# Weight preparation on three engines, centring products inside the GRU's last cells, and two alternating products in the last layer of a graph network kernel

## The reference

```python
agg = _prop_once(x, edge_attr, src, dst, ...) + _prop_once(x, edge_attr, dst, src, ...)
    # _prop_once: segment_sum(mlp3(concat(x[from], x[to], edge)), to), hidden width 256
s1 = _gru(x, agg, ...); s2 = _gru(agg, s1, ...); s3 = _gru(s1, s2, ...)
x = _layernorm(x + s3)
X = x
for l in range(3):
    S = segment_sum(X[src], dst)
    Z = (1.0 + eps[l]) * X + S
    H = relu(Z @ W1[l] + b1[l])
    X = H @ W2[l] + b2[l]
x = _layernorm(x + X)
```

## Time and profile before

| | us |
|---|---|
| median of 3 runs | 2313.74 (2311.68 to 2316.02) |
| the profiled execution | 2316.54 |
| its span | 2314.8 |
| busy PE / DVE / ACT / POOL | 2257.0 / 1762.0 / 1231.7 / 1182.7 |
| edge stage, from the span's start | about 1899 |
| GRU and first layer norm, until line 2136 starts | to 2025.9 |
| three layers and second layer norm | to 2314.8 |

### The profile page before, as it was taken

How to read it: one execution, slowest core, us unless ns; L and a number is a source line. 1 busy time by engine, 2 the same in 40 slices (tenths; PEclk the granted TensorE clock), 3 DMA queues, 4 the chain that set the end, 5 groups by cost and what they waited for, 6 DMA issues and landing times.

```text
span 2314.8 us, 38789 instructions
## 1 busy us (share of the span) xinstructions
PE 2257.0 (98%) x12559; PEld 1831.4 (79%) x12559; DVE 1762.0 (76%) x4035; ACT 1231.7 (53%) x2118; POOL 1182.7 (51%) x858
## 2 busy tenths in 40 slices
PE   4999999999999999999999999999999999899997
PEld 3888888888888888888888888888888874587775
DVE  7888888888888888888888888888888856703112
ACT  4565666566666656665666566656656543411122
POOL 2566666666566656665666666666656640001100
PEclk9999999999999999999999999999999999999999
DMA  4356454455445554554554445444545339286965
GB/s 163 71 113 125 98 106 92 88 112 101 91 89 106 99 98 91 108 97 89 100 112 93 88 98 107 99 89 104 101 89 99 72 62 268 94 351 258 384 263 189
DMA packets 242547, 292.52 MB, mean 126 GB/s; under 512 B 126757, under 2 KB 200056, under 8 KB 234385
## 3 DMA queue, kind: packets, MB, share of 16 engines
q1 hardware_dynamic: 168194, 236.50, 33.9%
q0 software_dynamic: 73216, 54.58, 18.0%
q10 hardware_dynamic: 1040, 0.52, 0.1%
HBM read 218.43 MB, written 73.08 MB: 126 GB/s over the span
## 4 chain that ended last, share of the span: by engine, by line
PE 92%; DMA 3%; DVE 2%; issue 1%; ACT 1%; POOL 0%; DVEq 0%; SPq 0%; POOLq 0%; ACTq 0%
PE bank L1238 24%; PE bank L1224 18%; PE bank L1250 16%; PE bank L2136 8%; PE bank L1303 4%; PE bank L1282 4%; PE bank L1298 4%; PE bank L1185 4%; DMA l_ring<-adj 2%; PE bank L1801 2%; PE bank L1267 2%; PE bank L1809 1%; PE bank L1268 1%; PE bank L2150 1%; PE bank L2159 1%
## 5 line engine op out<-in xcount | busy, mean ns | idle before, releaser
L495 POOL DMA_INDIRECT sums<-outb,target x416 | 667.3, 1604 | 590.8 <-ACT outb L666 456.8
L488 POOL DMA_INDIRECT xg<-in_x,gidx x416 | 489.3, 1176 | 148.3 <-issue 137.1
L1250 PEld LDWEIGHTS bank<-w3t,h 128*128 128x128 f32 x3328 | 387.5, 192 | 8.8 <-issue 0.2
L1250 PE MATMUL bank<-w3t,h 128*128 128x128 f32 x3328 | 388.3, 275 | 0.1
L1238 PE MATMUL bank<-h1h,w2h 128*128 128x512 f32 x832 | 365.5, 439 | 3.3 <-DVE h1l L861 3.3
L648 ACT ACTIVATE h<-bank,b2c 128x512 f32<-128x512 f32 x416 | 286.2, 688 | 122.2 <-PE bank L1238 122.2
L634 ACT ACTIVATE h1h<-hpre 128x512 fp32r<-128x512 f32 x416 | 257.8, 628 | 171.9 <-DVE hpre L857 171.9
L1238 PE MATMUL bank<-h1h,w2l 128*128 128x512 f32 x832 | 328.8, 395 | 0.0
L1238 PE MATMUL bank<-h1l,w2h 128*128 128x512 f32 x832 | 328.5, 395 | 0.0
L861 DVE SCALAR_TENSOR_TENSOR h1l<-hpre,h1h 128x512 fp32r<-128x512 f32 x416 | 268.6, 687 | 16.8 <-ACT h1h L634 16.8
L857 DVE TENSOR_TENSOR hpre<-pb,bank 128x512 f32<-128x512 f32 x416 | 264.9, 676 | 2.3 <-PE bank L1224 2.1
(11 more groups left out here) (263 smaller groups left out, 3695.6 us busy)
## 6 DMA issues: line engine op xcount, KB each, us to landing
l_ring<-adj SPq DMA_DIRECT2D x54, 1568.0 KB, 8.2
rowb<-along SPq DMA_DIRECT2D x104, 512.0 KB, 4.4
ef<-in_edge_attr SPq DMA_DIRECT2D x103, 256.0 KB, 2.7
adj<-band SPq DMA_DIRECT2D x46, 480.0 KB
adj<-band SPq DMA_DIRECT2D x23, 540.0 KB
stay<-adj SPq DMA_DIRECT2D x6, 1568.0 KB, 14.8
xg<-in_x,gidx POOLq DMA_INDIRECT x416
sums<-outb,target POOLq DMA_INDIRECT x416, 4.0
```

The lines of the kernel that those rows point to most:

```text
L488: pool.indirect_dma_start(out=to, out_offset=None, in_=a["x"], in_offset=bass.IndirectOffsetOnAxis(ap=ids, axis=0)).then_inc(s_x[par], 16)
L495: pool.indirect_dma_start(out=tables[k % 2], out_offset=bass.IndirectOffsetOnAxis(ap=target[par][:, 1, k:k + 1], axis=0), in_=outb[par][:, ...
L1250: last = nc.tensor.matmul(bank[6 + way][:, t * P:(t + 1) * P], h2[:, way, k, t * P:(t + 1) * P], w3t[:, k, :], start=not bias and k == 0, ...
```

## The change

Four edits. **Start:** `whalf` is computed by GpSimd ahead of its branch; ScalarE copies the upper parts and `w3t`, VectorE only subtracts; the four operations on `b3` go to the other program, which does not run here. In the windowed program SyncE loads `xw` ahead of `rowb`; VectorE does `sums(0)` and `lower_parts(0)` ahead of `pair_rows`, and `nodes(0)` and `compare(0)` behind `ways(0)`. **GRU:** the centring product of group n-2 stands in the last GRU's cell n, between its `h` products and its `hn`; it goes to bank 3 or 7, the one that `hn` of the cell before used, and ScalarE squares it and copies it to `x1` at once. Variance, root and scaling follow, the scaling now within `x1`; group 3 is scaled by GpSimd, group 5 by ScalarE. **Last layer:** TensorE alternates `unit(n)` (the first product of chunk n) with `second(n-1)`. **Store:** SyncE stores groups 0 and 1 apart.

```diff
-HALVES = ((0, 16, (0, 1, 2, 3)), (16, NB, (4, 5, 6)))
+NORMED = ((0, 16, (0, 1, 2, 3)), (16, NB, (4, 5, 6)))
...
                 for g in range(2):
+                    window(g, g)
                     everywhere(g, g)
-                for g in range(2):
-                    window(g, g)
...
+            pool.wait_ge(s_wload, 6 * 16)
+            for f in range(HB):
+                nc.gpsimd.tensor_tensor(whalf[:, f, 0, :], w1n[:, f, 0:D], w1n[:, f, D:2 * D], ALU.add).then_inc(s_wsum, 1)
+                nc.gpsimd.tensor_tensor(whalf[:, f, 1, :], w1n[:, f, 0:D], w1n[:, f, D:2 * D], ALU.subtract).then_inc(s_wsum, 1)
+            pool.wait_ge(s_wsum, 2 * HB)
+            nc.gpsimd.tensor_scalar(whalf, whalf, 0.5, None, ALU.mult).then_inc(s_whalf, 1)
...
+            for f in range(HB):
+                act.wait_ge(s_wT, 3 + f)
+                nc.scalar.copy(w1h[:, f, :, :].rearrange("p j m -> p (j m)"), bank[2 + f][:, 0:3 * P]).then_inc(s_wh, 1)
...
                 onehot(0, 0, 0)
                 window(0, 0)
+                sums(0)
+                lower_parts(0)
                 pair_rows()
-                sums(0)
-                nodes(0, 0, early=True)
-                lower_parts(0)
-                compare(0, 0, 0)
                 onehot(1, 1, 0)
                 window(1, 1)
                 ways(0)
+                nodes(0, 0, early=True)
+                compare(0, 0, 0)
...
+    def middle(j):
+        return bank[6 if j == NGR - 1 else 7 if j % 2 == 0 else 3]
...
+            if c == LAYERS - 1 and n >= 2:
+                square(n - 2)
             act.wait_ge(s_pre, seq + 1)
...
+            nc.scalar.activation(sqr[0:r, j % 2, 0:n], middle(j)[0:r, 0:n], ACT.Square).then_inc(s_sqd, 1)
+            nc.scalar.copy(x1[0:r, b:b + nb, :], middle(j)[0:r, 0:n].rearrange("p (b d) -> p b d", b=nb)).then_inc(s_cen, 1)
...
+        def back(j):
+            pe.wait_ge(s_zero, 4)
+            pe.wait_ge(s_cell, (LAYERS - 1) * NGR + j + 1)
...
+            if c == LAYERS - 1 and n >= 2:
+                pe.wait_ge(s_pre, seq)
+                back(n - 2)
+                if n >= 3:
+                    pe.wait_ge(s_cen, n - 2)
             nc.tensor.matmul(bank[4 * par + 3][:, 0:w], wt[:, c, 1, 2, :], chunk(h, n),
                              start=True, stop=True).then_inc(s_hn, 1)
...
+        pe.wait_ge(s_pre, LAYERS * NGR)
+        pe.wait_ge(s_cen, NGR - 3)
+        back(NGR - 2)
+        back(NGR - 1)
...
+            if j == 0:
+                pe.wait_ge(seam.s_cen, NGR)
...
+                    for n in range(NGR):
+                        unit(n)
+                        if n:
+                            second(n - 1, w2c[:, :])
+                    second(NGR - 1, w2c[:, :])
```

More of the change, by code:

```diff
@@ L1652, in square @@
                 act.wait_ge(s_red, j - 1)
[L1653 to L1667, removed]
+            b, nb = GROUPS[j]
+            r, n = rows_in(j), nb * D
+            nc.scalar.activation(sqr[0:r, j % 2, 0:n], middle(j)[0:r, 0:n], ACT.Square).then_inc(s_sqd, 1)
+            nc.scalar.copy(x1[0:r, b:b + nb, :], middle(j)[0:r, 0:n].rearrange("p (b d) -> p b d", b=nb)).then_inc(s_cen, 1)
+        for todo in seqs:
+            cell(*todo)
+        root(0)
+        square(NGR - 2)
+        square(NGR - 1)
+        root(1)
+        act.wait_ge(s_cen, NGR)
+        act.wait_ge(s_rstd, 2)
+        b, nb = GROUPS[NGR - 2]
+        for t in range(nb):
+            last = nc.scalar.activation(x1[:, b + t, :], x1[:, b + t, :], ACT.Identity, scale=stat[:, 3, b + t:b + t + 1])
+        last.then_inc(seam.s_norm2, 1)
     @block.vector
@@ L1719, in blend, with reduced, variance, inverse @@
                 nc.vector.tensor_tensor(chunk(out, n), diff[:, par, 0:w], chunk(xt, n), ALU.add).then_inc(s_cell, 1)
+        sums, var, std, rstd = (stat[:, j, :] for j in range(4))
+        def reduced(j):
+            b, nb = GROUPS[j]
+            r = rows_in(j)
+            dve.wait_ge(s_sqd, j + 1)
+            nc.vector.tensor_reduce(sums[0:r, b:b + nb], sqr[0:r, j % 2, 0:nb * D].rearrange("p (b d) -> p b d", b=nb),
+                                    axis=AX.X, op=ALU.add).then_inc(s_red, 1)
+        def variance(h):
+            lo, hi, js = NORMED[h]
+            dve.wait_ge(s_red, js[-1] + 1)
+            nc.vector.tensor_scalar(var[:, lo:hi], sums[:, lo:hi], 1.0 / D, EPS, ALU.mult, ALU.add).then_inc(s_var, 1)
+        def inverse(h):
+            lo, hi, js = NORMED[h]
+            dve.wait_ge(s_std, h + 1)
+            nc.vector.reciprocal(rstd[:, lo:hi], std[:, lo:hi]).then_inc(s_rstd, 1)
+        def scaled(j):
+            dve.wait_ge(s_rstd, 1 if j < 4 else 2)
+            dve.wait_ge(s_cen, j + 1)
+            b, nb = GROUPS[j]
+            r = rows_in(j)
+            part = x1[0:r, b:b + nb, :]
+            nc.vector.tensor_tensor(part, part, rstd[0:r, b:b + nb].unsqueeze(2).broadcast_to([r, nb, D]),
+                                    ALU.mult).then_inc(seam.s_norm, 1)
         sums_in(0)
@@ L1791, in sums_out @@
             last.then_inc(s_sumT, 1)
+        def back(j):
+            pe.wait_ge(s_zero, 4)
+            pe.wait_ge(s_cell, (LAYERS - 1) * NGR + j + 1)
+            b, nb = GROUPS[j]
+            r = rows_in(j)
+            for t in range(nb):
+                last = nc.tensor.matmul(middle(j)[0:r, t * D:(t + 1) * D], block_cols(aggt, b + t), cen[:, :],
+                                        start=True, stop=True)
+            last.then_inc(s_back, 1)
         def cell(c, n, seq):
@@ L1921, in _ @@
                     load(t, i)
+        sp.wait_ge(s_norm3, 1)
+        store(sp, 0, 1)
         sp.wait_ge(s_norm3, 2)
-        store(sp, 0, 2)
+        store(sp, 1, 2)
         sp.wait_ge(s_norm, 2)
@@ L2147, in program, with unit @@
                 panels(pe, product)
-                for n in range(NGR):
+                def unit(n):
                     pe.wait_ge(s_z, l * NGR + n + 1)
```

114 lines of the change are left out of this document (58 added, 56 removed).

## The result

| | median of the runs, us | ratio to before, 95% interval |
|---|---|---|
| before, 5 runs beside the change | 2313.74 | |
| after, 5 runs | 2323.92 (2321.88 to 2328.29) | 1.0049 [1.0038, 1.0060] |

The medians differ by 10.2 us; the interval stands for 8.8 to 13.9. The forecast was +7.5, or 2321.2, and its range of 2316.2 to 2326.0 holds the time. The profiled execution of the change took 2323.41 (span 2321.6) and stands 6.9 above that of before.

The account below looks back on a forecast made before the run. TensorE was taken to bound the kernel, with 92% of the chain of waits. Start 1.0, GRU 3.2 and last layer 3.3 made +7.5 us on the median of 2313.74, so 2321.2, range 2316.2 to 2326.0.

Parts of the forecast that it names:

- the cells: Sign in the profile: the last GRU's last cells take 6.1 us; the prediction is wrong if they stay at 5.2.
- the start of line 2113: Sign behind the GRU: this line's 50 instructions start about 3 us later relative to the GRU's start, at half clock.
- the forecast's own range: Whole kernel: 2318.5 to 2324 us for the forecast case, inside the full range of 2316.2 to 2326.0.
- The start: Tile 0: `ways(0)` 0.8 later by moving `pair_rows`, GpSimd's weights 0.2, removed VectorE work 0; +1.0 us in all.
- The GRU: Last GRU cells and their norm: longer cells, a later start of line 2113, the same 7.88 there; +3.2 us.
- cells 3, 4 and 5 are longer by 0.93 and by 0.1: Last GRU: centring group 0.93 and blend wait 0.1 per cell; VectorE's cell 5 comes 4.1 later, at 2009.1.
- GpSimd and VectorE within `x1`: GRU norm's scaling: each engine can hold up the other; GpSimd's 1.04 delays VectorE's second scaling, hidden under TensorE.
- The last layer: Last layer: ScalarE's first square waits for the seventh relu, 3.4 later, and VectorE's tail follows; +3.3 us, range +2.8 to +3.6.
- The clock did not stay up: Rival, chance 0.14: line 2113 runs at full clock, 5.9 instead of 7.88; GRU +0.8 instead of +3.2, total 2318.8.
- the gather came later and not earlier: Rival at the start, chance 0.12: rows land at 25 us, giving -4.2 there instead of +0.2; total 2316.8.
- the overlap did not work as meant: Rival, chance 0.04: cells not limited by TensorE, centring free, both norms end 4 us earlier; total 2309.
- The third rival: Chance 0.12: GpSimd ahead of `fits` gives +2.8 instead of +0.2, or lasting half clock GRU +6.6; either about 2324.3.

Follow-up runs that it names:

- Experiment 5: Kernel before with only the GRU's edits, the centring group placed behind `hn` instead of ahead of it: ratio 1.0007 [0.9997, 1.0017], +1.6 us.
- experiment 7: Kernel before with the last layer's alternation alone, and ScalarE's squares 0 to 3 between the relus: ratio 0.9996 [0.9987, 1.0004], -0.9 us.
- experiment 4: Kernel before with only the alternation of the two products in the last layer: ratio 1.0015 [1.0005, 1.0025], +3.5 us.
- experiment 8: Kernel before with 11, 10, 11 and 12 unread products in TensorE's pauses of the start: ratio 0.9988 [0.9979, 0.9997], -2.8 us.

## Why the prediction held, and where it did not

**Direction, places and range were right.** Each of the three parts is slower or neutral by itself, at the place that was named, and they add. Of the signs that the prediction named, `ways(0)` relative to `lower_parts(0)` (0.93 for 0.8), the pause ahead of group 4 (3.43) and the first square behind the seventh relu came true; the cells (6.48 for 6.1) and the start of line 2113 (5.7 for 3) did not. The measured 2323.92 lies at the very end of the forecast's own range, 2318.5 to 2324.

**The start** was forecast +1.0: 0.8 for `pair_rows` and 0.2 for GpSimd. The move cost 0.93 in the whole change and 0.6 alone. The rows came 0.82 late, not 0.2. The fourth gather's issue accounts for 0.34 of it; the rest is in the transfer, from that issue's end to the rows, which is 6.2 before, 6.7 after and 6.1 to 7.4 over the twelve traces, and stays open. GpSimd's scaling was priced at 0.9 and took 1.50, the four others 0.45 each, about as assumed; GpSimd ended at 16.54 for the forecast 16.0. `fits` itself came late too, for VectorE's little operations, which the prediction had running freely beside GpSimd. The gathers gained nothing from a quieter VectorE: the first of the four takes 1.20 to 1.26 in every trace and the fourth 0.94 or 0.95, whatever VectorE does. The VectorE work that was taken away is about 4.0 us in the timeline before (1.8 for `whalf`, 2.2 for the copies), not 1.9; it gives 0 all the same, for VectorE now waits 8.93 us ahead of `sums(0)`. The term's upper end (2.8) was not reached. The effect on the whole can't be resolved in time: +1.2 with an interval that holds zero, and the traces have the delay gone by the end of the edge stage.

**The GRU** was forecast +3.2 and cost 6.3 in the trace and 7.0 alone. The failed step is "cells 3, 4 and 5 are longer by 0.93 and by 0.1". The 0.93 was taken from 40 products in a row. A group that starts after a wait takes 1.13, and the rest of the loop is 0.2 longer than TensorE's cell had been, so a cell grew by 1.33 and VectorE's cell 5 came 5.3 later, not 4.1: 1.2 of the missing us. The loop had been seen ("TensorE is ready after 4.30 less what a semaphore takes"), but summed as TensorE's time plus a rest instead of going round it. Another 1.3 lie between blend 4 and the start of line 2113's products, which came 5.7 later for 3.2, and by the trace most of it is the clock: group 4 and the short `hn` were priced at full clock and changed to half within the group, so that VectorE waited 1.43 for that `hn` (the "issue" row, 0.8 more than forecast); groups 5 and 6 were priced between the two and went wholly at half (0.5 more). Half clock had been taken in full for the last 50 instructions alone; the same two pauses stand ahead of the 20 before them too. The last 0.6, the 8.46 for 7.88, is within what differs between executions. Experiment 5 shows that the order and not the added waits or the scaling made the loop: the same work with one block moved costs 1.6.

**GpSimd and VectorE within `x1`**, timeline:

```profile
2023.14 2.14 DVE L1772 TENSOR_TENSOR x<-x,g_stat 128x512 f32<-128x512 f32 x2
...
2023.18 1.55 POOL L1628 TENSOR_TENSOR x<-x,g_stat 128x512 f32<-128x512 f32 x1 [105.34 <-DVE g_stat L1764]
```

Two scalings take 2.14 instead of about 1.3 and GpSimd's 1.55 instead of the 1.04 of the earlier trace rows. VectorE's first began 0.04 ahead of GpSimd's; GpSimd's 1.55 is its 1.04 and what was left of that first one, and VectorE's second ends at 2025.28, 0.55 behind GpSimd's end. Each waited for the other's whole instruction, as the prediction had it. As forecast, this stayed off the chain: line 2175 waited for ScalarE's last copy, done at 2025.05. The Trainium skill (SBUF — State Buffer, "Who interferes with whom") says that a VectorE instruction with two SBUF inputs contends with a GpSimd instruction that reads SBUF. The trace agrees here, and at the start: the two-input operation of line 827, of two columns, took 0.37 beside GpSimd where the same one took 0.16 before. Line 830, longer by 0.22, has one such input, so this sentence does not cover it.

**The last layer** was forecast +3.3 and cost 3.1 in the trace, 3.5 alone; experiment 7 confirms the cause by taking it away.

**The rivals.** The clock did not stay up (line 2175 at 0.50), the gather came later and not earlier, the overlap did not work as meant. The third rival, GRU +6.6 by half clock throughout, named the right size for the GRU and half of the right reason; the loop's 1.2 was in no rival. The forecast of 7.5 against 10.2 owes little to cancelling: no term was much too large. That the time still fell inside the forecast's own range is in part luck, since nothing in that range allowed for the loop.

## What to carry to other kernels

Work that is moved ahead of an instruction for which another engine waits need not be overlapped: here it lengthened the loop between the two (6.48 for 5.15), and one place later it did so by no more than its own 0.89. Follow such a loop once around, each step with the length it has when it starts after a wait, and put the added work behind the instruction that the other engine waits for. When a producer's order is interleaved, its consumer's has to be too, and each piece of TensorE's work behind pauses like these (1.9 to 3.6 us) is priced at the lower clock. Before a trace's difference is given to an edit, look at the same stretch in traces that do not have the edit.

## What the runs showed of the hardware that was not expected

TensorE's clock falls also while TensorE is busy without a gap. In experiment 4's trace the stretches around the last layer's first products, with busy PE, PEld, DVE, ACT, POOL, then the granted clock:

```profile
2283.00:2287.00 4.00, 4.00 (x19) 3.19 (x18) 0.69 (x2) 0.00 (x0) 0.00 (x0) 1.00 0.00 0
2287.00:2289.00 2.00, 2.00 (x5) 0.88 (x4) 2.00 (x5) 0.00 (x0) 0.00 (x0) 0.65 0.00 0
2289.00:2291.00 2.00, 2.00 (x4) 0.81 (x3) 1.55 (x4) 0.69 (x1) 0.00 (x0) 0.50 0.00 0
```

Its first four products took 3.56 instead of 1.91 in experiment 7, and no other of the twelve traces has this stretch. Another one is in all twelve, between 1888 and 1904 us: TensorE is busy without a gap from 1888 to 1900, and the granted clock is 0.50 for a part of the time, of different length. From 1890 to 1900 it averages 0.66 in the kernel before, which is 3.4 us of work not done; in the change and in experiment 8 it is about 5.

The record of the clock isn't always to be trusted in the first stretch: for the kernel before, the row from 35 to 39 us reads 1.00, while the products of line 1224 start 0.43 apart, and 0.23 apart from 39 us on; in the change the same spacing stands under 0.50. So the spacing of equal instructions is the safer reading here.

Pauses at the start cost more than their own length, for the products behind them are slow: from 46 to 50 us the kernel before has 17 instructions at 0.50, experiment 8 has 25 at 1.00. Keeping TensorE busy with products that nobody reads won 2.8 us of 2314 there; no part of the change won anything that can be told from zero.
